# Group-norm attention on one core: the first group's products two tiles sooner, and one copy ahead of the exponentials on ScalarE

## The reference

```
h = group_norm(x, gn_w, gn_b)                      # 32 groups of 4 channels
q = einsum('bcn,oc->bno', h, wq) + bq
k = einsum('bcn,oc->bon', h, wk) + bk
v = einsum('bcn,oc->bno', h, wv) + bv
alpha = softmax(einsum('bnc,bcm->bnm', q, k) / sqrt(128))
out = einsum('bnc,oc->bon', einsum('bnm,bmc->bnc', alpha, v), wo) + bo
return out + x
```

## Time and profile before

| | |
|---|---|
| median of 3 runs | 223.59 us (222.37 to 223.93) |
| time of the profiled execution | 222.1 us |
| its span, first to last instruction | 220.4 us |
| PE busy | 203.2 us (92%) |
| DVE busy | 180.9 us (82%) |
| ACT busy | 177.3 us (80%) |
| POOL busy | 166.3 us (75%) |
| granted TensorE clock | 1.0 throughout |

### The profile page before, as it was taken

One profiled execution on the slowest core, in us unless ns is written; L12 is line 12 of the kernel. 1 busy time (PEld: TensorE's weight loads), 2 busy tenths in 40 slices (PEclk: granted clock), 3 DMA queues, 4 the chain that ended last, 5 costly groups with the idle time before them and its releaser, 6 DMA issues.

```text
span 220.4 us, 4306 instructions
## 1 busy us (share of the span) xinstructions
PE 203.2 (92%) x1513; PEld 139.9 (63%) x1513; DVE 180.9 (82%) x277; ACT 177.3 (80%) x279; POOL 166.3 (75%) x233
## 2 busy tenths in 40 slices
PE   0898679999999999999999999999999989998993
PEld 0764236767576756767576766667576657765993
DVE  1788999988889887989889897989877887788642
ACT  2259989998888889888998699888998888888820
POOL 6039996876889979997889949999689986795500
PEclk9999999999999999999999999999999999999999
DMA  5790999999999999999999999999999999999981
GB/s 160 231 400 18 190 161 225 188 179 226 201 204 195 229 171 212 247 178 189 202 174 249 187 224 212 229 174 223 209 171 219 182 227 196 187 192 205 276 304 51
DMA packets 135029, 44.61 MB, mean 202 GB/s; under 512 B 131168, under 2 KB 131936, under 8 KB 135008
## 3 DMA queue, kind: packets, MB, share of 16 engines
q1 hardware_dynamic: 134432, 44.08, 102.0%
q10 hardware_dynamic: 576, 0.26, 0.4%
HBM read 7.61 MB, written 4.22 MB: 54 GB/s over the span
## 4 chain that ended last, share of the span: by engine, by line
PE 75%; DVE 9%; issue 8%; ACT 5%; DMA 2%; SPq 0%; ACTq 0%; DVEq 0%
PE O L601 11%; PE O L603 10%; PE O L602 10%; PE S L570 10%; PE S L574 10%; PE S L572 10%; DVE neg_logits L911 5%; PE M L467 3%; PE M L466 3%; PE M L468 3%; DVE parts L927 2%; DMA x_sb<-in_x_dram 2%; ACT S L779 2%; ACT av L759 2%; ACT parts L790 1%
## 5 line engine op out<-in xcount | busy, mean ns | idle before, releaser
L911 DVE TENSOR_SCALAR_CACHE_REDUCE neg_logits<-S,c_tok 128x1024 f32<-128x1024 f32 x64 | 81.9, 1280 | 22.7 <-PE S L574 22.4
L779 ACT ACTIVATE S<-neg_logits,exp_bias 128x1024 f32<-128x1024 f32 x64 | 71.6, 1118 | 17.9 <-DVE neg_logits L911 17.7
L927 DVE SCALAR_TENSOR_TENSOR parts<-S,parts 128x1024 f16<-128x1024 f32 x64 | 78.0, 1219 | 1.7 <-ACT parts L790 1.3
L601 PE MATMUL O<-pT,v_hi 128*128 128x256 f16 x240 | 65.3, 272 | 3.7 <-ACT av L759 3.7
L790 ACT ACTIVATE parts<-S 128x1024 f16<-128x1024 f32 x64 | 65.4, 1022 | 1.6
L603 PE MATMUL O<-pT,v_lo 128*128 128x256 f16 x240 | 65.4, 272 | 0.0
L602 PE MATMUL O<-pT,v_hi 128*128 128x256 f16 x240 | 65.4, 272 | 0.0
L570 PE MATMUL S<-h_hi,u_hi 128*128 128x512 f16 x128 | 38.1, 379 | 2.4 <-DVE parts L927 2.4
L574 PE MATMUL S<-h_hi,u_lo 128*128 128x512 f16 x128 | 38.1, 379 | 0.0
L572 PE MATMUL S<-h_lo,u_hi 128*128 128x512 f16 x128 | 38.1, 379 | 0.0
L601 PEld LDWEIGHTS O<-pT,v_hi 128*128 128x128 f16 x240 | 24.3, 101 | 11.2 <-issue 4.9
(11 more groups left out here) (148 smaller groups left out, 287.4 us busy)
## 6 DMA issues: line engine op xcount, KB each, us to landing
x_sb<-in_x_dram SPq DMA_DIRECT2D x7, 512.0 KB, 8.4
inv_rows<-inv_line SPq DMA_DIRECT2D x6, 512.0 KB, 4.8
out_dram<-x_sb SPq DMA_DIRECT2D x6, 512.0 KB, 3.8
pT<-parts SPq DMA_TRANSPOSE x62, 4.8
out_dram<-x_sb SPq DMA_DIRECT2D x3, 256.0 KB, 4.7
x_sb<-in_x_dram SPq DMA_DIRECT2D x2, 256.0 KB, 3.9
out_dram<-x_sb SPq DMA_DIRECT2D x2, 128.0 KB, 1.9
inv_line<-row_inv SPq DMA_DIRECT2D x6, 4.0 KB, 2.0
```

Of the source, the lines that this page charges most:

```text
L601: nc.tensor.matmul(o, vh, ph, start=(m == 0), stop=False)
L779: nc.scalar.activation(S[T % 3][:, :], neg_logits[:, n % 2, :], ACT.Exp, scale=-1.0, bias=exp_bias[:, p, n:n + 1], accum_out=row_sum[:, p, ...
L911: nc.vector.tensor_scalar(neg_logits[:, n % 2, :], S[T % 3][:, :], c_tok[:, p, n:n + 1], None, ALU.add, ALU.min, accum_out=exp_bias[:, p, ...
L927: nc.vector.scalar_tensor_tensor(out=parts[:, T % SPLITS, N:2 * N], in0=S[T % 3][:, :], scalar=P_SCALE, in1=parts[:, T % SPLITS, 0:N], op0 ...
```

## The change

Two things change, and POOL's order with the first.

- The units of the first group run five tiles behind their logits (LEAD = 5): U0 to U3 stand behind L5 to L8, where they stood behind L7 to L10. Behind L9 and L10 no unit stands, and from L11 on all is as before.
- POOL makes the parts of the first image's v in the order that these units need: the second part of v directly behind the first, the third behind `u_parts(1, 0)`, and only then the second half of the next image's h (`h_parts(1, 1)`), which stood ahead of them.
- ACT copies a group's sums (`copy_values(b - 1, 1)`) in n = 6 ahead of that tile's exponentials, where it stood between the exponentials and the high part. This comes seven times. The copy of the other group, in n = 2, stays behind the exponentials.

```diff
+    LEAD = 5
...
         def unit_of(b, n):
 
-            past = TILES * b + n - LAG
+            T = TILES * b + n
+            past = T - (LEAD if T < LEAD + GT else LAG)
             return past // TILES, past % TILES // GT, past % GT
...
                 u_parts(b, 1)
-                if b + 1 < B:
+                if 1 <= b < B - 1:
                     h_parts(b + 1, 1)
                 row_bias(b, 2)
...
                 if b == 0:
                     v_parts(0, 0)
+                    v_parts(0, 1)
                     u_parts(1, 0)
+                    v_parts(0, 2)
+                    h_parts(1, 1)
...
-                v_parts(b, 1)
-                v_parts(b, 2)
+                if b >= 1:
+                    v_parts(b, 1)
+                    v_parts(b, 2)
...
-                    if TILES * b + n >= LAG:
+                    if LEAD <= TILES * b + n < LEAD + GT or TILES * b + n >= LAG + GT:
                         values(*unit_of(b, n))
...
+                    if n == 6 and b >= 1:
+                        copy_values(b - 1, 1)
                     exponentials(b, n)
                     if n == 2 and b >= 1:
                         copy_values(b - 1, 0)
-                    if n == 6 and b >= 1:
-                        copy_values(b - 1, 1)
                     high_part(b, n)
```

## The result

The changed kernel takes **220.08 us** (median of 4 runs, 219.25 to 221.33), the kernel before 222.98 us beside it (4 runs, 221.88 to 223.93): a ratio of 0.987, with a 95% interval of 0.983 to 0.992. The profiled execution took 219.72 us with a span of 218.0. All medians here are of all runs of a kernel, while the ratios leave out the runs that lay over 1.5% above the fastest of the same kernel, at most two of each, so a ratio is not always that of the medians.

What follows compares the result with a forecast made beforehand. PE was taken to bound the kernel from the second image on, waiting repeatedly only for ScalarE's copy; VectorE paced the ramp. Copy -4.8, end +0.1 and ramp +1.9 gave -2.8 us: 220.8 us as a median, range 218.6 to 223.3.

Steps and rivals of the forecast that it cites:

- The copy, -4.8 us: At n = 7, all seven PE waits on ScalarE's copy go, with 0.38 us to spare each: 4.8 us less.
- The estimate of 0.1 us at the end: At the program's end, the low part of T = 62, 0.25 us late, has thin cover: 0.1 us cost.
- The ramp, +1.9 us: Before PE runs dense: four units ahead of L9 delay VectorE, then the copy and U4; the ramp ends 1.9 us later.
- before 39.5, which was to refute the step: In the ramp: L9 was forecast 2.29 us late, at 40.03; a start before 39.5 would show that step wrong.
- I take this value: Ahead of U0: tile 1's transpose lands 6.3 us after issue, at 30.04, as in the profile before.
- the first sign of being right: Ahead of U0: a PE wait of about 1.1 us, put down to the transposes.
- No second wait: At U2: tile 3's transpose lands by 34.4 with the median 4.8 us, before U2 at 35.46, so PE does not wait.
- Zero, both ways: GpSimd's new order costs nothing: v parts done by about 25.6, h's second half at about 31.3, 5 us of cover.
- The transfer is there in time: Rival: tile 1's transpose lands in time, the ramp costs 0.8 us, the sum is -3.9, 219.7 us; chance 0.15.
- Interleaving pays: Rival: units fill PE's ramp gaps, nothing passed on; ramp gives -1.4, sum -6.1, 217.5 us; chance 0.09.
- The copy pays half: Rival: the copy starts later than forecast and PE still waits; half the gain, sum -0.4, 223.2 us; chance 0.17.
- slower: Rival: the exponentials' 0.60 us delay per copy is not absorbed; seven cost 4.2, sum +1.4, 225.0 us; chance 0.07.

Runs made afterwards that it cites:

- copy_only: Against the kernel before, only the n = 6 copy of the sums goes ahead of the exponentials; units and POOL's order as before: 219.65 us, ratio 0.984.
- copy_residual: copy_only with GpSimd's addition of the output bias moved behind the next iteration's first half of h: 218.98 us, ratio 0.982 to the kernel before.
- lead_only: The changed kernel with ScalarE's old order: first group's units two tiles sooner, POOL's new order, copy behind the exponentials: 224.87 us, ratio 1.007 to the kernel before.
- copy_pool: Against the kernel before: n = 6 copy ahead of the exponentials and GpSimd's new order, all units seven tiles behind: 219.93 us, ratio 0.984.
- lead5_two: The changed kernel, but only U0 and U1 moved forward; U2 and U3 stay behind L9 and L10: 220.18 us, ratio 0.987 to the kernel before.
- after_first_copy: The changed kernel with the first group's copy (T = 10) also ahead of that tile's exponentials: 220.67 us, ratio 0.988 to the kernel before.
- both_ahead: Against the kernel before, both copies (n = 2 and n = 6) ahead of the exponentials in every image, nothing else: 219.64 us, ratio 0.987.
- best: copy_residual with GpSimd's new order and no unit moved: 220.85 us, ratio 0.986 to the kernel before.
- copy_behind_high: Against the kernel before, the n = 6 copy goes behind the high part, nothing else changed: 230.40 us, ratio 1.034.

## Why the prediction was right, point by point

**The time.** Forecast was 2.8 us less; measured were 2.9 in the medians, 2.4 in the profiled executions and 2.7 from L5 on. The total agrees better than its terms do, and that part is luck: by the steps between PE's starts the copy gave 4.8, the ramp cost 1.5 and not 1.9, the end cost nothing and not 0.1, and 0.8 that the sum did not have was lost in the seventh image.

**The copy, -4.8 us.** Right as a term: 4.8 us of waits went, and the 0.20 us to the copy's start, the 0.6 of the exponentials and the 0.25 of the low part are all in the rows of T = 14. The step of 0.72 from the copy's start to PE is found again at U4 (46.79 to 47.51). But I went through the cover of ScalarE and VectorE only. GpSimd was not on the list of who must keep up when PE is 0.65 us sooner per image, and in the seventh image it couldn't, held up by the broadcast and with the addition still ahead of h: 0.8 us came back (`copy_only` shows it, `copy_residual` removes it). The estimate of 0.1 us at the end did not show: from the last logits to the end it is 18.0 us against 18.8, so the last wait's 0.8 us was gained whole.

**The ramp, +1.9 us.** The way is right, and the price about: U4 is 1.5 us late in the changed kernel, 1.9 in `lead_only`, and against `copy_pool`, which has GpSimd's order but no unit moved, the changed kernel's U4 is 20.64 - 18.64 = 2.0 us late. L9 came 1.86 us late instead of 2.29; at 39.89 it is not before 39.5, which was to refute the step. VectorE passed the delay on, and PE waited 1.35 us for the unmoved copy, forecast at 1.4. `lead5_two`, in which L9 is not late, has no loss in the ramp. Two steps in it failed. "I take this value" for the landing of tile 1: it landed after 4.4 us, not 6.3, so U0 did not wait, and the first sign of being right, a wait of about 1.1 us there, did not show. And "No second wait" at U2: the transposes of tile 3 took 5.9 us and not the median 4.8, so the wait came there, with nearly the same length. The forecast of where was wrong, and the sum was saved by the one taking the place of the other. That was luck of the forecast, but no accident of one execution. In 13 of the 14 profiled executions of this study tile 1 landed after 4.4 to 5.0 us and tile 3 after 5.4 to 6.4; the exception in both is the one profile of the kernel before (6.3 and 4.7), from which the prediction was made. All four executions with U2 behind L7 waited ahead of U2, for 1.0 to 1.5 us. And I named the copy as what holds U4; it does, but `after_first_copy` shows that moving it gives nothing, since VectorE is as late by then.

**GpSimd's order, "Zero, both ways".** Wrong by 0.5 us to the good, as `copy_pool` shows: `u_lo` no longer lies across `spread`, which VectorE, the pace-setter there, has to finish first. The estimates themselves held: both parts of v were done at 25.85 (forecast 25.6) and the second half of h at 31.68 (31.3).

**The rivals.** "The transfer is there in time" was half true, and did not bring its price, since the next transfer was not. "Interleaving pays" has fallen with `lead_only`. "The copy pays half" and "slower" have fallen with `copy_only` and `both_ahead`.

**What stays open.** Why `best` isn't faster than `copy_residual` is argued from one profile: its waits for `u_lo`, `spread` and the last transposes are seen, but why the same transposes take 4.7 us in one execution and 6.4 in another was not tried. Only the two kernels with GpSimd's new order and no unit moved have them late (6.0 and 6.4; at most 5.1 in the other twelve profiles), so it may belong to that order rather than to chance; with one profile of each this is not shown. Nor was it tried why tile 1 and tile 3 land as they do, nor what makes the stretch before L5 differ.

## What to carry to other kernels

A wait that repeats once per stage on the engine that bounds the kernel is worth its steps between starts, not only the idle time that the view shows; and one queue position on the engine that it waits for may remove it. Before work is moved forward to fill an idle stretch of the engine that bounds the rest of the kernel, look which engine sets the pace in that stretch: where it is another one, the moved work comes back as that engine's delay. When the bounding engine gets faster, check every engine that feeds it, also the one with the lowest busy share, for the one stretch in which it is just in time. And a duration that decides a step of a forecast, above all that of a transfer, should be read in more than one execution: here the only profile at hand was the exception for both transfers that mattered.

## What the runs showed of the hardware

The VectorE operation `spread` on 128 x 1 elements took 0.22 us or up to 1.49. It runs 112 times in the 14 profiles; in 66 it took over 0.25 us, and each of these ended within 0.03 us behind the end of a GpSimd operation, which in 62 of them had begun before it. (In the other four, in `copy_behind_high`, it began 0.05 us after it, while the last 0.08 us of the GpSimd operation ahead of it lay over the start.) In the kernel before (VectorE, then GpSimd):

```profile
27.61 0.73 DVE L872 SCALAR_TENSOR_TENSOR spread<-dmean,mv 128x1 f32<-128x1 f32 x1
```

```profile
27.17 1.16 POOL L355 TENSOR_TENSOR u_lo<-u,u_hi 128x512 f16<-128x512 f32 x1
```

Both end at 28.33 to 28.34. The longest, in `best`, ran from 145.35 to 146.84 beside an `attn` from 145.31 to 146.83. In the changed kernel, beside the shorter `v_hi` (27.69 to 28.09), it took 0.22, its time alone, and ended 0.03 behind it:

```profile
27.90 0.22 DVE L878 SCALAR_TENSOR_TENSOR spread<-dmean,mv 128x1 f32<-128x1 f32 x1
```

The Trainium skill, SBUF — State Buffer, section "SBUF: two separate sides", says that VectorE with two SBUF inputs and a reading GpSimd share one pair of ports, and that whoever starts first holds it for the whole instruction. The ends that fall together agree with that; the four cases in which the GpSimd operation began 0.05 us after `spread` do so only if `spread` still stood behind the one before. The large low parts of VectorE, which have one input in PSUM, took 1.21 to 1.23 us each, in all 14 profiles, whatever GpSimd did.

The second surprise is how one kind of transfer varies. The same transpose of tile 1 landed after 6.3 us in one execution and after 4.4 in another, with the same instructions ahead of it on its queue, and all 62 lie between 4.2 and 7.2. Much of this belongs to the place in the program and not to chance: besides tile 3 (5.4 to 6.4 us in 13 of 14 profiles), that of tile 51 took 7.0 to 7.2 us in 13 of 14, and 5.7 in `copy_behind_high`.
